# Self-attention values copied straight from PSUM by ScalarE, their bias added once through the output weights

## The reference, cut to what matters

```
x = x + cross_attention(layernorm(x), ctx)      # 64 queries, 256 keys, 16 heads of 16
x = x + self_attention(layernorm(x))            # 64 queries, 64 keys, causal, 16 heads of 16
x = x + ffn(layernorm(x))                       # weights and activations quantized, 256 to 1024 to 256
```

```
qkv = x @ w_qkv + b_qkv
q, k, v = jnp.split(qkv, 3, axis=-1)
q, k, v = (heads(q), heads(k), heads(v))
att = jnp.einsum('bhqd,bhkd->bhqk', q, k) / jnp.sqrt(jnp.float32(D_HEAD))
att = jax.nn.softmax(jnp.where(causal, att, -jnp.inf), axis=-1)
y = jnp.einsum('bhqk,bhkd->bhqd', att, v)
return y.transpose(0, 2, 1, 3).reshape(B, T, C) @ w_out + b_out
```

## Time and profile before

| | |
|---|---|
| Time, median of 3 runs | 884.32 us (883.75 to 885.76) |
| The profiled execution | 883.71 us |
| Its span, first to last instruction | 881.7 us |
| Mean granted TensorE clock | 0.996 of full speed |
| Cross-attention | to about 525 us |
| Self-attention | about 525 to 745 us |
| FFN | the rest |

### The profile page before, as it was taken

How to read it: one execution, slowest core, us unless ns; L and a number is a source line. 1 busy time by engine, 2 the same in 40 slices (tenths; PEclk the granted TensorE clock), 3 DMA queues, 4 the chain that set the end, 5 groups by cost and what they waited for, 6 DMA issues and landing times.

```text
span 881.7 us, 28587 instructions
## 1 busy us (share of the span) xinstructions
PE 850.0 (96%) x9750; PEld 714.4 (81%) x9750; DVE 756.1 (86%) x1583; ACT 693.2 (79%) x2045; POOL 482.8 (55%) x710
## 2 busy tenths in 40 slices
PE   7999999999999999999999988999999998999997
PEld 6889888898888888988888867888888875666664
DVE  6888888888888888888888877999999988999995
ACT  4778887777777777787777765888888877999996
POOL 4433234355554555334433327878787864777775
PEclk9999999999999999999999998999999999999999
DMA  4351110111011111111111000000000000000011
GB/s 135 116 175 50 48 42 30 50 44 48 30 42 48 38 46 35 42 48 33 39 48 36 13 2 1 2 3 1 0 1 0 1 3 1 31 31 30 30 36 36
DMA packets 31635, 31.84 MB, mean 36 GB/s; under 512 B 3280, under 2 KB 30800, under 8 KB 31568
## 3 DMA queue, kind: packets, MB, share of 16 engines
q1 hardware_dynamic: 30448, 30.47, 11.0%
q10 hardware_dynamic: 1120, 0.59, 0.2%
HBM read 26.86 MB, written 4.19 MB: 35 GB/s over the span
## 4 chain that ended last, share of the span: by engine, by line
PE 78%; ACT 12%; issue 5%; DVE 2%; POOL 2%; DMA 0%; DVEq 0%; ACTq 0%; POOLq 0%; SPq 0%
PE psum L353 12%; PE psum L310 9%; PE psum L324 9%; PE psum L340 8%; PE psum L380 7%; PE psum L688 5%; ACT probs L1063 4%; PE psum L726 3%; PE psum L737 3%; PE psum L389 3%; PE psum L364 3%; ACT probs L520 3%; PE psum L297 2%; PE psum L780 2%; PE psum L707 2%
## 5 line engine op out<-in xcount | busy, mean ns | idle before, releaser
L520 ACT ACTIVATE probs<-psum,nmax 128x256 f32<-128x256 f32 x512 | 235.6, 487 | 57.0 <-DVE nmax L477 56.8
L551 POOL TENSOR_TENSOR rm<-rinv,hm_sb 128x256 f32<-128x256 f32 x64 | 39.7, 620 | 260.6 <-DVE rinv L449 260.6
L477 DVE TENSOR_REDUCE nmax<-psum 128x2 f32<-128x512 f32 x256 | 159.0, 684 | 11.6 <-PE psum L340 11.4
L353 PE MATMUL psum<-id_sb,probs 128*128 128x128 f32 x1024 | 126.4, 275 | 0.9
L353 PEld LDWEIGHTS psum<-id_sb,probs 128*128 128x128 f32 x1024 | 114.3, 141 | 4.3 <-ACT probs L520 4.2
L520 ACT ACTIVATION_READ_ACCUMULATOR probs<-psum,nmax 128x1 f32 x512 | 112.3, 219 | 0.0
L544 POOL TENSOR_TENSOR cl<-c_sb,ch 128x512 fp32r<-128x512 f32 x64 | 81.8, 1278 | 10.0 <-ACT ch L495 9.2
L340 PE MATMUL psum<-k_sb,qb 32*128 32x256 f32 x1024 | 75.1, 401 | 2.3 <-DVE qb L433 1.2
L528 POOL TENSOR_TENSOR rstd<-vare,minus_half 128x1 f32<-128x1 f32 x96 | 53.4, 556 | 36.3 <-DVE vare L410 32.5
L340 PEld LDWEIGHTS psum<-k_sb,qb 32*128 32x128 f32 x1024 | 47.0, 184 | 21.3 <-issue 17.8
L899 POOL TENSOR_TENSOR w_all<-c_sb,qm_sb 128x1024 f32<-128x1024 f32 x32 | 60.6, 1895 | 3.1 <-ACT c_sb L844 3.1
(11 more groups left out here) (162 smaller groups left out, 2502.6 us busy)
## 6 DMA issues: line engine op xcount, KB each, us to landing
c_sb<-in_ctx_t SPq DMA_DIRECT2D x64, 256.0 KB, 2.8
x_sb<-in_x SPq DMA_DIRECT2D x32, 128.0 KB, 2.5
out<-y_sb SPq DMA_DIRECT2D x32, 128.0 KB, 1.7
w_all<-in_w_gate SPq DMA_DIRECT2D x1, 1024.0 KB, 5.1
w_all<-in_w_up SPq DMA_DIRECT2D x1, 1024.0 KB, 6.6
w_all<-in_w_down SPq DMA_DIRECT2D x1, 1024.0 KB, 6.4
wqkv_sb<-in_w_qkv SPq DMA_DIRECT2D x1, 768.0 KB, 6.9
wk_sb<-in_wk ACTq DMA_DIRECT2D x1, 256.0 KB, 4.1
```

What stands on the lines that cost most here:

```text
L353: last = nc.tensor.transpose(sp[g][:, c:c + P], probs[:, 2 * g + u, kh * P:(kh + 1) * P], id_sb[:])
L477: nc.vector.tensor_reduce(nmax[:, 2 * g:2 * g + 2], sp[g].rearrange("p (u s) -> p u s", u=2), AX.X, ALU.max, negate=True).then_inc(max_don ...
L520: nc.scalar.activation(probs[:, j, :], sp[g][:, u * S:(u + 1) * S], ACT.Exp, bias=nmax[:, j:j + 1], accum_out=rsum[:, j:j + 1]).then_inc(e ...
```

## The change

ACT reads the values from PSUM itself and DVE's add goes. `v2` exists twice, one for even and one for odd tiles, so ACT's copy of tile t waits for the product of tile t-2 and no more for that of t-1. In ACT's order the copies for tile t+1 now open `body2(t)`; those for tiles 0 and 1 stand ahead of the first tile. PE's waits for DVE's add become waits for ACT's fourth copy. The bias is multiplied once by the output weights, in tile 8 of the cross-attention, and added to `bout_sb`; for this DVE spreads it over `oT2` ahead of the tile.

```diff
-        bv2_sb = sb("bv2_sb", [P, D])
+        bv2_sb = sb("bv2_sb", [P, KT])
...
-        v2b = [sb(f"v2b{s}", [P, D]) for s in range(2)]
-        v2 = sb("v2", [P, 2, D])
+        v2 = [sb(f"v2{s}", [P, 2, D]) for s in range(2)]
...
         def pe_v2(pe, t, s, j):
             pe.wait_ge(xl_done, t + 1)
-            pe.wait_ge(v2b_done, t)
+            pe.wait_ge(v2_ev, t * 4)
...
-        def dve_v2(v, t, par):
-            v.wait_ge(v2_mm, t + 1)
-            if not isinstance(t, int) or t > 1:
-                v.wait_ge(v2_ev, t * 4 - 4)
-            nc.vector.tensor_tensor(v2b[par][:], v2_ps, bv2_sb[:], ALU.add).then_inc(v2b_done, 1)
+        bias_ps = mp[:, 0:D]
+
+        def dve_bias_rows(v):
+            v.wait_ge(w2_in, 16 * len(SET2))
+            nc.vector.tensor_copy(oT2[:], bv2_sb[:].unsqueeze(2).to_broadcast([P, KT, P]))\
+              .then_inc(bias_set, 1)
+
+        def pe_bias(pe, t, n):
+            pe.wait_ge(bias_set, 1)
+            pe.wait_ge(qb_done, n * 4 + 4)
+            pe.wait_ge(x1h_done, t + 3)
+            for k in range(KT):
+                last = nc.tensor.matmul(bias_ps, oT2[:, k, :], wout_sb[:, k, :],
+                                        start=k == 0, stop=k == KT - 1)
+            last.then_inc(bias_mm, 1)
+
+        def dve_bias(v):
+            v.wait_ge(bias_mm, 1)
+            nc.vector.tensor_tensor(bout_sb[:], bias_ps, bout_sb[:], ALU.add).then_inc(bias_done, 1)
...
         def act_v2(a, t, par):
-            a.wait_ge(v2b_done, t + 1)
-            a.wait_ge(pv2_mm, t)
+            a.wait_ge(v2_mm, t + 1)
+            if t > 1:
+                a.wait_ge(pv2_mm, t - 1)
             for i in range(2):
                 for hh in range(2):
                     nc.scalar.activation(
-                        v2[half(hh), i, :].rearrange("p (j h e) -> p j h e", h=2, e=E)[:, :, hh, :],
-                        v2b[par][half(i), :].rearrange("p (j h e) -> p j h e", h=2, e=E)[:, :, hh, :],
+                        v2[par][half(hh), i, :].rearrange("p (j h e) -> p j h e", h=2, e=E)[:, :, hh, :],
+                        v2_ps[half(i), :].rearrange("p (j h e) -> p j h e", h=2, e=E)[:, :, hh, :],
                         ACT.Copy).then_inc(v2_ev, 1)
...
                     pe_scores(pe, t, 1, n, j)
+                    if wsum:
+                        pe_bias(pe, t, n)
                     pe_r(pe, t, 0)
...
                     if wsum:
                         pe.wait_ge(wscale, 1)
+                        pe.wait_ge(bias_done, 1)
                     pe_pv(pe, t, 0, j)
...
                 pe_q2(pe, 0, 0)
-                pe.wait_ge(v2b_done, 1)
+                pe.wait_ge(v2_ev, 4)
                 pe_xt2(pe, 2, x0_ps)
...
                 pe_scores2(pe, 0, 0, 0, 0)
-                pe.wait_ge(v2b_done, 2)
+                pe.wait_ge(v2_ev, 8)
                 pe_xt2(pe, 3, x0_ps)
...
                     if ahead5:
-                        pe.wait_ge(v2b_done, t + 2)
+                        pe.wait_ge(v2_ev, (t + 2) * 4)
                         pe_xt2(pe, t + 5, x0_ps)
...
                     if scale:
                         dve_wscale(v)
+                        dve_bias(v)
...
+                dve_bias_rows(v)
                 body(8, 4, 0, scale=True)
...
                 act_k2(a, 0, 0)
+                a.wait_ge(const_set, 4)
+                act_v2(a, 0, 0)
                 act_pt(a, t, 1)
...
                 act_r(a, t, 1)
+                act_v2(a, 1, 1)
                 act_xt2(a, 3, 1, 1, x0_ps)
...
                 def body2(t):
-                    act_v2(a, t, t % 2)
+                    if t > 0:
+                        act_v2(a, t + 1, (t + 1) % 2)
...
                 act_xqt(a, 1)
-                act_v2(a, NT - 1, 1)
                 act_r2(a, NT - 1)
...
                 pool_xl(p, 3, 1, 1)
+                p.wait_ge(bias_done, 1)
                 for i in range(4):
                     pool_xb2(p, i)
```

More of the change, by code:

```diff
@@ L208, in block_kernel @@
         SET2 = [(wqkv_sb[:], k_of(w_qkv)), (bqk_sb[:], b_qk),
-                (bv2_sb[:], on_all(b_v2)), (wout_sb[:], k_of(w_out)),
+                (bv2_sb[:], b_v2), (wout_sb[:], k_of(w_out)),
                 (bout_sb[:], on_all(b_out)), (qm4_sb[:], q_mask4),
@@ L641, in block_kernel @@
         v2_ev = sem("v2_ev")
-        v2b_done = sem("v2b_done")
+        bias_set = sem("bias_set")
+        bias_mm = sem("bias_mm")
+        bias_done = sem("bias_done")
         kbd4_pool = sem("kbd4_pool")
@@ L750, in pe_r2, with pe_pv2 @@
             last.then_inc(r2_mm, 1)
-        def pe_pv2(pe, t):
+        def pe_pv2(pe, t, par):
             pe.wait_ge(v2_ev, t * 4 + 4)
@@ L763, in pe_pv2 @@
                             o2_ps[32 * c:32 * c + 32, m, i * L:(i + 1) * L],
-                            v2[:, i, 32 * j:32 * j + 32], p2T[:, at_p, i * L:(i + 1) * L],
+                            v2[par][:, i, 32 * j:32 * j + 32], p2T[:, at_p, i * L:(i + 1) * L],
                             start=True, stop=True)
@@ L1295, in body2 @@
                         pe_v2(pe, t + 2, there, i % 2)
-                    pe_pv2(pe, t)
+                    pe_pv2(pe, t, i % 2)
                 for t in range(4):
@@ L1314, in _ @@
                 pe_xq(pe, 0)
-                pe_pv2(pe, t)
+                pe_pv2(pe, t, 0)
                 pe.wait_ge(wq_step, 36)
@@ L1319, in _ @@
                 pe_gate(pe, 0, 0)
-                pe.wait_ge(v2b_done, NT)
+                pe.wait_ge(v2_ev, 4 * NT)
                 pe.wait_ge(xh_done, NT)
@@ L1331, in _ @@
                 pe_gate_up(pe, 1)
-                pe_pv2(pe, t)
+                pe_pv2(pe, t, 1)
                 pe_out2(pe, t)
@@ L1354, in _ @@
                 nc.vector.memset(ones[:], 1.0).then_inc(const_set, 1)
-                nc.vector.memset(v2[:], 0.0).then_inc(const_set, 1)
+                for w in v2:
+                    nc.vector.memset(w[:], 0.0).then_inc(const_set, 1)
                 nc.vector.memset(eps_col[:], EPS).then_inc(const_set, 1)
@@ L1446, in _ @@
                   .then_inc(b_set, 1)
-                dve_v2(v, 0, 0)
                 dve_stats(v, LN2, 3, at(3))
@@ L1452, in _ @@
                 dve_o(v, t, 1)
-                dve_v2(v, 1, 1)
                 dve_stats(v, LN2, 4, at(4))
@@ L1488, in body2 @@
                         dve_xn(v, LN2, t + 6, at(t + 6), xt2_mm)
-                    if t + 2 < NT:
-                        dve_v2(v, t + 2, t % 2)
                 for t in range(NT):
@@ L1590, in _ @@
                 act_xt2(a, 4, 0, 0, x0_ps)
-                a.wait_ge(const_set, 3)
                 a.wait_ge(op_done, 2 * NT)
                 def body2(t):
-                    act_v2(a, t, t % 2)
+                    if t > 0:
+                        act_v2(a, t + 1, (t + 1) % 2)
                     if 0 < t < NT - 1:
@@ L1782 @@
             a["L0_xattn_Wo"].T, a["L0_xattn_bo"], a["L0_attn_w_qkv"], per_partition(a["L0_attn_b_qkv"][:2 * D]),
-            a["L0_attn_b_qkv"][2 * D:],
+            per_partition(a["L0_attn_b_qkv"][2 * D:]),
             a["L0_attn_w_out"], a["L0_attn_b_out"], a["L0_ffn_w_gate"].T, a["L0_ffn_w_up"].T,
```

## The result

The changed kernel takes **886.12 us** (median, 884.48 to 889.27), the kernel before on the same chip 884.25 (882.50 to 887.02), 22 runs each: a ratio of **1.0022, 95% interval 1.0014 to 1.0030**. The change costs 1.9 us. I had put it at 884.24, no change, with 882.5 to 885.8 as the range and a chance of 0.07 on slower by over 0.2%: wrong in sign and size. The profiled execution after has a span of 883.5 us where the one before had 881.7.

What follows compares the result with a forecast made beforehand. The prediction took TensorE (PE) as the bound, with savings on DVE worth something only at the self-attention's ends. It summed 0.87 + 0.13 + 0 - 0.84 - 0.24 = -0.08 on 884.32, so 884.24 us, range 882.5 to 885.8.

Steps and rivals of the forecast that it cites:

- Bias at tile 8, +0.87: Cross-attention, tile 8: four new PE matmuls for the bias count in full, +0.87 us.
- the cover: Cross-attention, tile 8: PE's new wait for DVE's finished bias is hidden with 0.47 us to spare; up to +0.4 if not.
- Into the self-attention, +0.13: Start of self-attention: PE's transpose of tile 3 waits for ACT's four value copies, +0.13 us; bounds 0 and +0.8.
- Steady tiles, 0: The 26 middle self-attention tiles: PE sets their length, so relieving DVE changes nothing, 0; bounds down 0.3, up 0.
- rival E: Steady self-attention tiles get shorter, 0.1 us a tile, -2.6 in all: 881.7 us; chance 0.06.
- rival D: ACT's strided PSUM reads are slow, at twice the length 0.4 us for each of 26 tiles: 894 us; chance 0.03.
- Out of the self-attention, -0.84 - 0.24 = -1.08: Last self-attention tiles: three lost DVE adds at 0.28 us give -0.84; ACT's dropped copies ahead of the FFN give -0.24.
- A: Self-attention's end gives nothing back, the add sat in slack; +1.0 in all, 885.3 us; chance 0.20.
- B: Self-attention's end gives more, all four adds and ACT's copies nearly whole, -2.7: 882.4 us; chance 0.15.
- PE gains four instructions: Sign in the later profile: one new group of 128x256 f32 matmuls at cross-attention tile 8, no PE idle time behind it.
- The score matmuls stay 6.23 us apart: Sign in the later profile: the self-attention tile period stays 6.23 us; any other period refutes the whole sum.
- Rival C: Shifted waits bring a second half-clock stretch of PE at the self-attention's start: 886.3 us; chance 0.06, 0.04 of it slower.

Runs made afterwards that it cites:

- e4: Kernel before with 5 one-column memsets more at the head of DVE's stream; 884.78 us, ratio 1.0009 to before.
- e1: Changed kernel with 992 unused bytes per partition behind `bv2_sb`, so later tensors have their old place modulo 64; 885.12 us, ratio 1.0007 to before.
- e2: Kernel before with 32 unused bytes per partition behind `bv2_sb`, giving later tensors the changed kernel's place modulo 64; 885.60 us, ratio 1.0019 to before.
- p2: Kernel before with only the split context tensors `ch` and `cl` moved by 32 bytes modulo 64; 887.28 us, one execution.
- p3: Kernel before with 32 bytes ahead of the first weights only; no total given, cross-attention 137.27 and 351.76 us, steady tiles 163.49 us.
- e3: Changed kernel with 11 one-column memsets more at the head of DVE's stream; 885.26 us, ratio 1.0008 to before.
- f2: Changed kernel with 11 memsets more on DVE and cross-attention weights placed at 0, self-attention weights, `ch`, `cl` at 32 modulo 64; 882.14 us, ratio 0.9983 to before.
- f1_again: Second measurement of the changed kernel with the 992 unused bytes and the 11 memsets; 883.11 us, ratio 0.9988 to before.
- p4: Kernel before with only the tensors from `probs` on moved by 32 bytes; 887.08 us, one execution.
- p1: Kernel before with 32 unused bytes ahead of the first weights and 32 behind `bv2_sb`; 887.96 us, one execution.
- f1: Changed kernel with both the 992 unused bytes behind `bv2_sb` and the 11 memsets on DVE; 882.95 us, ratio 0.9981 to before.

## Why the prediction was wrong, step by step

- **Bias at tile 8, +0.87.** Right: +0.86. The chain of waits (start, duration, what), answering to the earlier trace rows, has the new product at 154.18 and PE without a gap behind it:

```profile
154.18 1.06 PE psum L836 x4
155.24 0.22 PE psum L363 x2
...
158.45 1.80 PE psum L352 x16
160.25 1.01 PE psum L379 x32
```

The piece grew by 0.86, though the chain gives the product 1.06. DVE's add (L842) ended at 159.86, and PE took up the product with the values at 160.25 straight behind the transposes: the cover held. DVE's timeline, answering to the earlier trace rows:

```profile
151.03 0.20 DVE L448 RECIPROCAL rinv<-rsum 128x8 f32<-128x8 f32 x1 [0.39 <-ACT probs L519]
...
158.37 0.69 DVE L419 TENSOR_TENSOR v_s<-psum,bv_sb 128x512 f32<-128x512 f32 x1 [0.75 <-PE psum L323]
...
159.46 0.40 DVE L842 TENSOR_TENSOR bout_sb<-psum,bout_sb 128x256 f32<-128x256 f32 x1
159.78 1.28 DVE L441 COPY hq_all<-psum 128x512 f32<-128x512 f32 x2
```

- **Into the self-attention, +0.13.** Not seen. "Into" falls into three groups, by how long the lower clock lasts in it, and in each it isn't longer with the change: without such a stretch at 525 to 537 us 38.14 and 38.19 against 38.29 (e4); with a short one 39.62 (e1) against 39.49 to 39.87 (e2, before, p2, p3); with one twice as long 40.76 to 40.91 (e3, f2, f1_again) against 40.77 and 40.83 (p4, p1). Within a group they spread by up to 0.4, more than the 0.13. The link itself is sharper: from the last value matmuls to the transpose of tile 3 it is 1.67 us in before (534.83 to 536.50) and 1.67 in after (537.73 to 539.40 below). I had priced a copy from PSUM like one from SBUF, 1.30 for the four. They take 1.16 (ACT's timeline, to be read against the earlier trace rows):

```profile
538.16 1.16 ACT L879 ACTIVATE v<-psum 64x128 f32<-64x128 f32 x4 [0.47 <-PE psum L708]
```

That ends at 539.32. PE has the first tile's scores between those values and the transpose of tile 3, until 539.47, and starts the transpose at 539.40 without idle time (PE's timeline). So the term was nothing, the lower bound of the prediction, "0 if each copy from PSUM is 0.04 shorter":

```profile
537.73 0.40 PE L708 MATMUL psum<-w2h,cl 128*128 128x256 f32 x2
538.06 0.39 PE L720 MATMUL psum<-ca_b,id_b 64*128 64x512 bf16 x2
538.38 1.09 PE L727 MATMUL psum<-w_all,qT 64*64 64x256 f32 x16
539.40 0.44 PE L680 MATMUL psum<-id_sb,xn 128*128 128x128 f32 x2
```

The rule of the Trainium skill (VectorE: DVE Perf Modes, The TRN2 errata) that I had weighed and set aside, 43 ns more for an SBUF source by estimate, is near what the 64x128 copies show: 308 less 272 is 36 ns. The 128x256 rows that I took against it differ in the type of their output as well.

- **Steady tiles, 0.** Right for the work moved, wrong for the time. f1 (162.85) and e4 (162.84), alike in placement and in having no stall, agree within 0.01 with and without the change. So rival E, a steady tile that gets shorter by the relieved engines, is refuted too; and rival D, slow strided reads of PSUM, falls with the 272 ns per copy. The measured -1.16 is placement, -0.82 (after against e1), and the stall, -0.34.
- **Out of the self-attention, -0.84 - 0.24 = -1.08.** Mechanism right, size too small: -1.34 (32.53 to 32.57 in all kernels with the change, 33.87 to 33.93 in all without). The chain keeps its links (DVE's sum, POOL, ACT, PE's projection), answering to the earlier trace rows; the add of the values that the chain before has at 732.75 is in it no more. Three links of before that neither nor the earlier trace rows shows, and then the chain after:

```profile
712.74 1.20 DVE rsum L798
...
719.58 1.22 DVE rsum L798
...
734.84 0.94 PE psum L780 x6
```

```profile
714.57 1.20 DVE rsum L799
...
721.09 1.22 DVE rsum L799
...
727.11 1.20 DVE rsum L799
...
730.27 0.96 PE psum L781 x6
...
733.90 0.37 DVE oT L814
...
735.67 0.94 PE psum L781 x6
...
746.39 1.10 PE psum L774 x4
```

After is 1.83 us behind before at the first of these (714.57 to 712.74), then 1.51 (721.09 to 719.58), 1.16 (730.27 to 729.11), 0.83 (735.67 to 734.84) and 0.47 (746.39 to 745.92). Three drops of 0.32 to 0.35 stand where I had taken 0.28 for each of three adds, and one of 0.36, over the last tile with ACT's dropped copies, where I had 0.24: that is most of the 0.26 beyond the forecast. (Which instruction gave each drop is my reading of the order; no run took the adds out one by one.) By the prediction's own marks (under 0.4 for A, over 1.8 for B) rivals A and B are both refuted.
- **The step that failed** is a term put at nothing without a reason: that what the change doesn't touch keeps its time. The sum had no term for the cross-attention outside tile 8 and none for the FFN, and 0 for the steady tiles. "PE gains four instructions" and "The score matmuls stay 6.23 us apart" supposed that a matmul costs the same wherever its operands lie, and that DVE's instructions cost the same wherever they stand in its stream. The diff showed the shrunken `bv2_sb`; I read it as a smaller load. It cost +2.5 in the cross-attention and -0.8 in the steady tiles. The 59 instructions taken from DVE's stream cost +1.4 in the FFN and -0.34 in the steady tiles. Together +2.8, against -0.5 from the change's own work: bias +0.86, into 0, steady 0, tail -1.34. The sum, +2.3, stands beside +2.42 by the profiles and +1.87 by the medians (interval 1.2 to 2.7).
- **Rival C** gave 886.3, near the measured 886.12, by a mechanism that didn't act: it wanted a second low-clock stretch, and the profile of after has less low clock than that of before ("into" is 1.55 shorter); such a stretch comes and goes between executions of one kernel. A time that fits is no proof of the reason behind it.

## What to carry to other kernels

A diff that resizes a tensor or drops an instruction moves everything behind it: look at the distance between the addresses of matmul operands and at the streams' counts before crediting or blaming the work itself. When stages that the change doesn't touch change their time, cut both timelines at the same instructions, stage by stage, and restore placement and position one at a time. A kernel whose gain is below 0.3% should be compared with the by-products held fixed; here that turns a loss of 1.9 us into a lower median, by 0.5 and by 1.3 us.

## What the runs showed of the hardware

- In the cross-attention's values' product, steps of two matmuls of 128x128 by 128x256 with fp32r operands start 233 to 236 ns apart when the addresses of stationary and moving operand in SBUF differ by 32 bytes modulo 64 (either way round), and 240.0 ns apart when the distance is a multiple of 64 (in these runs of 256 too). In the self-attention's values' product, of the same size and roles, the operands that agree modulo 64 (64 apart modulo 128) are the quicker ones: 20.67 to 20.76 us in 26 tiles, against 20.89 to 21.02. So the modulus isn't shown, and 64 is the one that it can't be for both.
- That isn't all of the steady tiles' gain. Their keys' and queries' projections (weights stationary, L689 in after) take 38.2 to 38.5 us of PE's time in after, e2, e3 and p2, and 38.9 to 39.3 in all other kernels, p1 and f2 among them, whose operands are as far apart modulo 128 as those of after. So p2 and e2 gain 0.8 us in the steady tiles against before (163.18), p1 only 0.35, and f2 only 0.33 over f1_again. Why is open.
- DVE stalls about 0.3 us at places 128 records of its stream apart (seen four times in a row in the FFN of after, three times in e4). Where in the tile the stall falls decides whether anyone waits for it: in the FFN a shift by 5 instructions was worth 1.05 us (e4 less before), one by 11 was worth 1.38 (after less e3) and 1.50 (e1 less f1). The profile lays it to the engine of the last semaphore. What DVE does in that time no row shows.
- The first transfer's landing (4.09 to 5.47 us over 13 profiles), a low-clock stretch at 8 to 12 us in three of them (1.3 us more before the first scores) and the one between the stages ("into" 38.19 and 40.91 us for one kernel) move the span from execution to execution: f1 and f1_again, the same kernel, have 879.9 and 882.1 us, a difference larger than all that the change did.
